# Ternary stage: the shift of x on ScalarE, its rounding behind VectorE's third butterflies

## What is computed

```python
def act_quant(x, bits=8):
    qb = float(2 ** (bits - 1))
    scale = qb / jnp.clip(jnp.max(jnp.abs(x), axis=-1, keepdims=True), EPS)
    xq = jnp.clip(jnp.round(x * scale), -qb, qb - 1) / scale
    return x + jax.lax.stop_gradient(xq - x)
def bitlinear(x, w):
    return jnp.einsum('bsh,oh->bso', act_quant(x), weight_quant(w))
def h_bitlinear(x, w):
    return jnp.einsum('bsh,oh->bso', act_quant(fwht(x)), weight_quant(w))
gate = bitlinear(x, w_gate)
up = bitlinear(x, w_up)
intermediate = jax.nn.silu(gate) * up
return h_bitlinear(intermediate, w_down)
```

## Time and profile before

| | |
|---|---|
| median of 3 runs | 1864.46 us (1863.8 to 1865.15) |
| profiled execution | 1866.64 us |
| its span, first to last instruction | 1864.8 us |
| TensorE busy (matmuls) | 1622.4 us, 87% |
| VectorE busy | 1306.6 us, 70% |
| ScalarE busy | 938.4 us, 50% |
| GpSimd busy | 676.8 us, 36% |
| mean granted TensorE clock | 0.943 of 2.4 GHz |

### The profile page before, as it was taken

The page is one execution under the profiler, slowest core; times in us unless marked ns, Lnnn a source line. Parts: engine busy times, 40 slices in busy tenths (PEclk is TensorE's granted clock), DMA queues, the critical chain, the costliest instruction groups (busy, mean ns, idle before and its releaser), DMA issues. The chain is left out here.

```text
span 1864.8 us, 26347 instructions
## 1 busy us (share of the span) xinstructions
PE 1622.4 (87%) x8780; PEld 1143.6 (61%) x8812; DVE 1306.6 (70%) x2366; ACT 938.4 (50%) x1932; POOL 676.8 (36%) x634
## 2 busy tenths in 40 slices
PE   7999958899856799996589989999869989999995
PEld 5788845555524456565466656566637767677774
DVE  6476645666858899995467476685847979876674
ACT  3232215776655566654356456464625545655552
POOL 4044406676512232331222122221303215555563
PEclk9999988999978899998899989999889989999998
DMA  6200017533020000000512112121114110000000
GB/s 203 69 23 1 0 42 204 162 113 98 17 92 1 1 1 1 1 1 3 162 40 72 49 46 69 34 69 52 52 44 143 58 34 1 1 23 1 24 23 23
DMA packets 66848, 95.71 MB, mean 51 GB/s; under 512 B 12176, under 2 KB 28688, under 8 KB 66716
## 3 DMA queue, kind: packets, MB, share of 16 engines
q1 hardware_dynamic: 58460, 80.40, 13.9%
q0 software_dynamic: 6144, 12.60, 2.5%
q10 hardware_dynamic: 2112, 1.05, 0.2%
HBM read 56.25 MB, written 4.19 MB: 32 GB/s over the span
## 5 line engine op out<-in xcount | busy, mean ns | idle before, releaser
L2560 PE MATMUL bank<-fp_xT,fp_weights_values 128*128 128x512 f32 x704 | 186.8, 405 | 12.4 <-DVE fp_gate L2460 10.9
L1477 ACT ACTIVATE causal_probs<-bank,causal_neg 128x512 f32<-128x512 f32 (+3 forms) x256 | 134.1, 530 | 116.5 <-DVE causal_neg L1569 74.1
L2560 PEld LDWEIGHTS bank<-fp_xT,fp_weights_values 128*128 128x128 f32 x704 | 132.0, 192 | 55.1 <-DVE fp_gate L2460 18.0
L774 DVE TENSOR_REDUCE heads_neg<-bank 128x1 f32<-128x512 f32 x128 | 87.2, 681 | 76.6 <-PE bank L820 76.3
L744 ACT ACTIVATE heads_probs<-bank,heads_neg 128x512 f32<-128x512 f32 x128 | 88.1, 689 | 102.6 <-DVE heads_neg L774 102.5
L2585 PE MATMUL bank<-fp_wd,fp_hT 128*128 128x512 f32 x528 | 133.3, 393 | 5.3 <-DVE X L2482 3.5
L1368 POOL DMA_DIRECT2D causal_qS<-causal_qk x96 | 48.1, 509 | 230.6 <-DVE causal_qk L1527 230.6
L2469 DVE SCALAR_TENSOR_TENSOR fp_up<-bank,fp_weights_scales,fp_up 128x512 f32<-128x512 f32 x132 | 99.1, 751 | 44.3 <-ACT fp_up L2366 37.4
L922 POOL TENSOR_TENSOR ternary_z<-ternary_z 128x1024 f32<-128x1024 f32 x16 | 37.7, 2356 | 217.7 <-DVE ternary_z L1069 217.7
L2585 PEld LDWEIGHTS bank<-fp_wd,fp_hT 128*128 128x128 f32 x528 | 98.5, 188 | 29.5 <-issue 7.7
L1165 PE MATMUL bank<-weights_raw,ternary_qT 128*128 128x512 bf16 x433 | 107.8, 396 | 7.2 <-ACT weights_raw L611 3.6
(11 more groups left out here) (276 smaller groups left out, 4146.1 us busy)
## 6 DMA issues: line engine op xcount, KB each, us to landing
heads_xd<-X SPq DMA_DIRECT2D x64, 128.0 KB, 2.7
heads_cd<-in_ctx SPq DMA_DIRECT2D x64, 128.0 KB, 2.8
causal_qS<-causal_qk SPq DMA_DIRECT2D x96, 64.0 KB, 2.8
causal_qS<-causal_qk POOLq DMA_DIRECT2D x96, 64.0 KB, 2.5
causal_kS<-causal_qk SPq DMA_DIRECT2D x96, 64.0 KB, 2.6
causal_kS<-causal_qk POOLq DMA_DIRECT2D x96, 64.0 KB, 2.5
X<-in_x SPq DMA_DIRECT2D x4, 1024.0 KB, 6.8
heads_cT<-in_ctxT SPq DMA_DIRECT2D x4, 1024.0 KB, 5.6
```

The lines of the kernel that those rows point to most:

```text
L774: dve.tensor_reduce(neg[:, g % 2, k:k + 1], banks[n % 3][:], AX, ALU.max, negate=True).then_inc(neg_ready, 1)
L1477: act.activation(probs_of(i)[:, h + one], view[:, one], ACT.Exp, bias=neg[:, G % 2, at:at + 1], accum_out=total[:, G % 2, at:at + 1]).then ...
L2560: last = pe.matmul(banks[4 + g][:], values[:, g, n % NI, of], xT[:, part, g], start=part == 0, stop=part == 1)
```

## The change

In `ternary_ffn` the shift of x, q32 = x * rate + ROUND, is taken out of VectorE's `quantized` and becomes a ScalarE operation, `shifted(t + 1)`, behind silu 2 and ahead of the evictions of y. It waits for the rate (`rated`) and for the rounding of the tile before (`q_ready`), which reads the same buffer. VectorE's rounding becomes a function of its own, `rounded`, and stands behind the third butterflies. In step 0 the quantization now stands ahead of the rounding of weight chunk 7 and `rounded(1)` behind it.

```diff
+            def shifted(t):
+                i = t % NT
+                act.wait_ge(rated, t + 1)
+                if t:
+                    act.wait_ge(q_ready, t)
+                act.activation(q32[:], norm.tile(0, t), ACT.Copy, scale=rate[:, i:i + 1], bias=ROUND).then_inc(q_shifted, 1)
+
             def step(t):
                 silus(t, 0)
                 silus(t, 1)
@@ -1002,6 +1009,8 @@
                 silus(t, 2)
+                if tile(t + 1):
+                    shifted(t + 1)
                 if tile(t - 2):
                     for c in range(CH):
                         act.wait_ge(y_ready, CH * (t - 2) + c + 1)
@@ -1046,8 +1055,10 @@
                 dve.tensor_scalar(rate[:, i], peak[:, i], QB, None, ALU.mult).then_inc(rated, 1)
-                dve.wait_ge(rated, t + 1)
-                dve.tensor_scalar(q32[:], x, rate[:, i], ROUND, ALU.mult, ALU.add).then_inc(q_shifted, 1)
+
+            def rounded(t):
+                if not tile(t):
+                    return
                 dve.wait_ge(q_shifted, t + 1)
                 if t >= 2:
                     dve.wait_ge(q_turned, t - 1)
@@ -1101,8 +1112,9 @@
                 z_chunk(t, 0)
                 if t == 0:
+                    quantized(1)
                     round_weights(7)
-                    quantized(1)
+                    rounded(1)
                 butterfly_stage(t - 1, 0)
                 z_chunk(t, 1)
@@ -1112,6 +1124,8 @@
                 if t:
                     quantized(t + 1)
                 butterfly_stage(t - 1, 2)
+                if t:
+                    rounded(t + 1)
```

## The result

The changed kernel takes **1884.23 us** as a median (1881.46 to 1884.84) against 1864.79 (1863.8 to 1865.15): a ratio of 1.0102, with an interval of 1.0085 to 1.0120. It is slower by 1.0%, some 19 us (19.4 by these medians); the forecast was 14.8 us slower. The profiled execution has a span of 1882.1 us, 17.3 more than before.

A forecast was written before the change was run, and what follows sets the result against it. VectorE was taken to set the pace, TensorE close behind. 11.4 us (late y eviction) + 3.7 (late power) - 0.3 (start-up) = +14.8 us, so 1864.46 + 14.8 = 1879.3 us, 0.8% slower; range 1870.5 to 1884.

The forecast's parts named there:

- The bound and the removed work: Ternary stage: VectorE sets the pace at 18.28 us a tile; removing its shift saves it 0.65 us a tile.
- The chain: Rate, ScalarE's shift, eviction of y0, y3, gate group, z3: each of 11 steps 1.04 us longer, 11.4 us.
- the second term: GpSimd's power falls behind VectorE's rounding of y and delays line 201: 0.37 us a tile, ten times, 3.7 us.
- The relief of VectorE: Rival: late evictions of y harmless, VectorE's 0.65 us a tile gained; 1857.0 us, or 1860.5 if TensorE binds; chance 0.05.
- The rival with the order on GpSimd kept: Same lengthening through y's evictions, but the power stays ahead of the rounding: +11.1 us, 1875.6 us; chance 0.22.
- The start-up: Steps -1 to 3: +0.25, +0.62, +0.1 and -1.3 us, in sum -0.3 us.
- step 4: First of the regular loop steps 4 to 14: forecast 1.04 us longer, with a TensorE gap of about 1.5 us.
- the clock rival: TensorE's new gap lowers its clock, one group of eight matmuls a tile at 1.2 GHz: 20.8 us more, 1900.1; chance 0.05.

The follow-up runs named there:

- round_back: The changed kernel with VectorE's rounding of x put back right behind the rate, ahead of the third butterflies; 1883.61 us, ratio 1.0100.
- wait_only: The kernel before, with ScalarE only waiting for the next tile's rate behind its third silu, nothing moved or added; 1874.58 us, ratio 1.0051.
- rate_round_scale: The changed kernel with the rate ahead of the second butterflies, rounding ahead of the third, line 201 behind the next step's z0; 1857.02 us, ratio 0.9955.
- scale_late: The changed kernel with VectorE's scaling of X (line 201) moved behind z0 of the next step; 1874.86 us, ratio 1.0058.
- start_only: The changed kernel with the change only in steps -1 to 3 (tiles 0 to 4), later tiles as before; 1861.85 us, ratio 0.9991.
- steady_only: The changed kernel with the change only from step 4 on (tiles 5 to 15), earlier tiles as before; 1883.57 us, ratio 1.0094.
- scale_late_before: The kernel before, with VectorE's scaling of X (line 201) moved behind z0 of the next step; 1861.34 us, ratio 0.9975.
- after_first_y: The changed kernel with ScalarE's shift behind the first eviction of y instead of ahead of it; 1865.72 us, ratio 1.0011.
- double_shift: The changed kernel with ScalarE's shift of x run twice at its place, first into an unread buffer; 1892.17 us, ratio 1.0154.

## Why the prediction was right, and where it was short

The direction, the mechanism and the place were right. The size was short by 4.2 us in the stage and by 4.6 between the medians: the median lies at the upper end of the range, 0.2 us above it.

**The bound and the removed work.** Right. VectorE's 0.65 us went into its wait ahead of z3: forecast 1.7, measured 1.73, and `round_back` shows that this is slack.

**The chain.** Right in the order of its links and in what each waits for; two of them were sized too small. Its length from the end of the rate to z3 is 735.92 - 731.58 = 4.34 us, forecast 4.21, so the tile pays 1.17 and not 1.04. The shift takes 0.72 us as taken; the two short ones are the hand-over from ScalarE to TensorE (732.85 to 732.97, 0.12 and not 0.06) and y3 with its way to the gate group (733.94 - 732.97 = 0.97 and not 0.89). The first was read from another pair of engines (VectorE to TensorE, after 0.33 us of waiting), the second from four groups in one piece. The waits themselves are longer than forecast, ScalarE's 3.26 us instead of 2.9 and TensorE's 1.80 instead of 1.5: the second term delays the rate and not TensorE, whose groups of y start 729.68 - 728.34 = 1.34 us ahead of z2 instead of 703.38 - 702.41 = 0.97.

**The second term.** Right to the hundredth: line 1143 follows z3 by 719.73 - 716.11 = 3.62 us, line 201 the rounding by 723.36 - 721.69 = 1.67. 18.28 + 1.17 + 0.37 = 19.82. The rule of the Trainium skill (SBUF — State Buffer, "Who interferes with whom") fits in that the power ends only behind VectorE's rounding, 723.32 against 722.92; it adds 0.40 us behind it, less than its whole length (0.55 us for the shortest power in this stage before), so by the rule alone the term would have come out too large. For the ordinary tile the prediction had the rule say why, and there it fits less well: whoever issues first has the ports and the other waits, but the power starts first, at 713.98, and the rounding behind it takes the same 1.23 us as in the tile where it starts first. The rows show when the power ends, not what holds it.

**The rivals.** The relief of VectorE needed 1.7 us of slack in y3's way to z3, and fell as there is none: in `wait_only` a gap of 1.2 us ahead of y3 already lengthens the tile. The rival with the order on GpSimd kept is out too, as the power starts 0.14 us behind the rounding. The advice of the Trainium skill (Perfetto Trace Analysis, "Optimizing Scalar/DVE Operations") to offload a saturated VectorE holds in `rate_round_scale` and fails in the change as made: the same operation on the same engine, with its operand there in time or not.

**The start-up** is the term that failed, -0.3 forecast and +1.55 measured. The instructions at its beginning came as sized: the fourth gate group of step 0 starts 547.18 - 525.08 = 22.10 us after the first maximum of x, against 547.83 - 526.63 = 21.20 before, 0.90 later for a forecast of 0.25 + 0.62. What the forecast had at nothing is TensorE's clock. Rows of TensorE in the changed kernel in steps 0, 3 and 4:

```profile
547.18 2.97 PE L1179 MATMUL bank<-weights_raw,ternary_qT 128*128 128x512 bf16 x8 [2.56 <-ACT weights_raw L611]
...
595.12 3.62 PE L1197 MATMUL bank<-eye,ternary_z 128*128 128x128 f32 x16
598.54 2.15 PE L1179 MATMUL bank<-weights_raw,ternary_qT 128*128 128x512 bf16 x7
...
632.19 1.13 PE L1209 MATMUL bank<-ternary_had,ternary_zT 128*128 128x128 f32 x8 [2.94 <-ACT ternary_y L1019]
633.15 3.57 PE L1179 MATMUL bank<-weights_raw,ternary_qT 128*128 128x512 bf16 x8
```

and the first two places in the kernel before:

```profile
547.83 1.90 PE L1165 MATMUL bank<-weights_raw,ternary_qT 128*128 128x512 bf16 x8 [1.91 <-ACT weights_raw L611]
...
595.45 2.85 PE L1183 MATMUL bank<-eye,ternary_z 128*128 128x128 f32 x16
598.14 1.89 PE L1165 MATMUL bank<-weights_raw,ternary_qT 128*128 128x512 bf16 x7
```

Eight matmuls take 1.9 us at 2.4 GHz and 3.6 at 1.2; the 2.97 of step 0 is a group in which the level rose. The differences are 1.07 us there and 0.77 + 0.26 in step 3, together 2.1, for the 1.85 that the forecast missed.

This isn't a fixed price of the change. `scale_late` has the same instructions in the same order up to z3 of step 3 (line 201 first stands behind this point in both), and there the level rose sooner:

```profile
547.89 2.53 PE L1179 MATMUL bank<-weights_raw,ternary_qT 128*128 128x512 bf16 x8 [2.52 <-ACT weights_raw L611]
...
595.58 2.53 PE L1197 MATMUL bank<-eye,ternary_z 128*128 128x128 f32 x16
```

It reaches this z3 after 83.48 us, as the kernel before does (83.50). So with the new start-up the traces show 85.05, 85.13 (`start_only`) and 83.48, with the old one 83.50, 83.42 (`steady_only`) and 83.48 (`scale_late_before`). Whether the change makes the late rise more frequent, three traces of each can't tell; it stays open.

In **step 4** the forecast left TensorE's gap at 1.5 us; it is 2.94, as z2 comes 2.49 us behind the start of TensorE's groups of y there and 1.34 in a regular tile. The gate group behind it ran at 1.2 GHz, 3.57 - 1.89 = 1.68 us more: the clock rival, once. `steady_only` has the same gap and not the fall:

```profile
633.60 1.13 PE L1220 MATMUL bank<-ternary_had,ternary_zT 128*128 128x128 f32 x8 [2.94 <-ACT ternary_y L1022]
634.57 1.89 PE L1190 MATMUL bank<-weights_raw,ternary_qT 128*128 128x512 bf16 x8
```

In `round_back` it is the same: a gap of 2.94 us and a group of 1.89. What decides it stays open. The 19 us of the result against 14.8 are thus 10 x 0.13 in the regular tiles, less 0.5 that one tile of before had lost to a late power already, 1.85 at the start, 0.96 in step 4 and 0.63 at the stage's end. In that last stretch the instructions are the same in all kernels that leave line 201 in its place, and it took from 45.8 (`after_first_y`) to 48.1 us (`double_shift`), again with TensorE's level rising at different places: its first 16 transposes of z took 3.62 us in the changed kernel, 3.03 before and 2.72 in `after_first_y`. So the 0.63 can't be put down to the change.

## What to carry to other kernels

Moving work to an engine with room is free only if its operand is there when its turn comes: an engine that executes in order pays for the wait with everything queued behind it, here an eviction whose bank another engine needs. The moved work, free where it finds its operand there, then adds its own length as well. Ask of each new wait what is queued behind it and when its releaser runs, and move the releaser ahead as well. And an engine that is relieved shows the next limits at once (a late q, a late sum, a power behind a rounding), so the gain has to be read against each of them.

## What the runs showed of the hardware

- A gap of 2.4 us on TensorE in every tile left its clock at 2.4 GHz (`double_shift`), while a single gap of 2.94 us was followed by a group at 1.2 GHz in one kernel and not in two others.
- The same instructions, from the first maximum of x to z3 of step 3, took 85.05 and 85.13 us in two executions and 83.48 in a third, as TensorE's level rose at other places: 16 transposes of z took 3.62 us in the first two and 2.53 in the third. A difference of 1.6 us in a stage with waits on TensorE can be the clock alone.
- GpSimd's power of 128x1 takes 1.32 us if it starts 0.06 us ahead of a 1.23 us rounding on VectorE, and 1.49 if it starts 0.14 behind it; a shift of 0.2 us in its start changes the tile by 0.37, enough to make tiles of 17.78 and 18.01 us alternate.
- After a gap of 1.80 us TensorE's group of y (eight records of 128x128) takes 0.97 us to the next group instead of 0.89.
